# Attention scores of two heads side by side in the two halves of TensorE's rows, with six of nine part products, and weights staged outside the probabilities

## What is computed

```python
# attention, 16 heads of 8 channels, causal
q, k, v = x @ Wq.T, x @ Wk.T, x @ Wv.T            # split into heads
attn = softmax(where(causal, q @ k.T * 8 ** -0.5, -inf))
x = layernorm(x + (attn @ v) @ Wo.T)
# mixture of experts: 64 experts of inner width 64, 8 groups of 8
scores = sigmoid(x @ router_w.T); sfc = scores + e_bias
# sum of the top 2 of each group -> best 4 groups -> best 8 experts of those
w = scores[topk] / (sum + 1e-20) * 2.5            # coefficients, zero elsewhere
moe = sum_e ((silu(x @ Wg[e]) * (x @ Wu[e]) * coef[e]) @ Wd[e])
shared = (silu(x @ SWg) * (x @ SWu)) @ SWd        # inner width 128
x = layernorm(x + moe + shared)
```

## Time and profile before

| | before |
|---|---|
| median of 3 runs | 962.97 us (962.12 to 964.05) |
| the profiled execution's own time | 962.95 us |
| its span, from the first to the last instruction | 961.2 us |
| mean granted TensorE clock | 0.993 |
| busy: PE, DVE, ACT, POOL | 98%, 78%, 49%, 62% of the span |

### The profile page before, as it was taken

One profiled execution on the slowest core, in us unless ns is written; L12 is line 12 of the kernel. 1 busy time (PEld: TensorE's weight loads), 2 busy tenths in 40 slices (PEclk: granted clock), 3 DMA queues, 4 the chain that ended last, 5 costly groups with the idle time before them and its releaser, 6 DMA issues.

```text
span 961.2 us, 16058 instructions
## 1 busy us (share of the span) xinstructions
PE 940.5 (98%) x5012; PEld 574.7 (60%) x5012; DVE 752.1 (78%) x2374; ACT 468.0 (49%) x866; POOL 597.8 (62%) x651
## 2 busy tenths in 40 slices
PE   9899999999999999999999999999999999999996
PEld 4355466666666666666666656666666655666663
DVE  4776877799877997789967997789877997478655
ACT  2355445455555545555455545555455555543221
POOL 2343147765777757776766757776676767775653
PEclk9799999999999999999999999999999999999999
DMA  8551144432643253423633345323634223242431
GB/s 287 171 160 62 49 158 138 135 107 87 205 133 116 91 182 114 135 78 114 214 125 101 105 159 160 111 81 97 211 112 124 93 103 113 88 144 77 160 109 55
DMA packets 64340, 121.70 MB, mean 127 GB/s; under 512 B 6656, under 2 KB 36224, under 8 KB 63744
## 3 DMA queue, kind: packets, MB, share of 16 engines
q1 hardware_dynamic: 64256, 120.67, 39.1%
HBM read 98.37 MB, written 22.02 MB: 125 GB/s over the span
## 4 chain that ended last, share of the span: by engine, by line
PE 85%; DVE 7%; DMA 3%; issue 2%; POOL 1%; ACT 1%; SPq 0%; POOLq 0%; DVEq 0%
PE acc L844 12%; PE ob L785 7%; PE sm L755 7%; PE st L773 7%; PE pg L714 6%; PE pu L714 6%; PE pg L716 5%; PE pg L715 5%; PE pu L716 5%; PE pu L715 5%; PE acc L710 4%; PE acc L829 3%; PE acc L831 2%; PE acc L830 2%; PE ob L797 2%
## 5 line engine op out<-in xcount | busy, mean ns | idle before, releaser
L958 POOL TENSOR_TENSOR hid<-hid,coef_b 128x512 f32<-128x512 f32 x240 | 309.4, 1291 | 158.5 <-DVE hid L1215 99.6
L1147 DVE CUSTOM_DVE_ANT_0 max_out<-sm,causal_sb 128x128 bf16<-128x128 f32 (+3 forms) x512 | 236.0, 485 | 58.0 <-PE sm L755 54.0
L907 ACT ACTIVATE hid<-pg 128x512 f32<-128x512 f32 x243 | 145.4, 598 | 209.7 <-PE pg L716 203.4
L879 ACT ACTIVATE probs<-st 128x512 f32<-128x512 f32 (+1 forms) x384 | 194.5, 525 | 93.6 <-PE st L773 90.3
L1206 DVE SCALAR_TENSOR_TENSOR hid<-hid,pg 128x512 f32<-128x512 f32 x243 | 165.3, 680 | 54.4 <-ACT hid L907 53.2
L1215 DVE TENSOR_TENSOR hid<-hid,pu 128x512 f32<-128x512 f32 x235 | 160.3, 682 | 40.7 <-PE pu L716 37.9
L962 POOL TENSOR_TENSOR hid_lo<-hid,hid_hi 128x512 fp32r<-128x512 f32 x112 | 144.4, 1290 | 64.9 <-ACT hid_hi L914 64.3
L944 POOL TENSOR_SCALAR_AFFINE_SELECT probs<-probs 128x256 f32<-128x256 f32 x256 | 98.4, 410 | 61.5 <-ACT probs L879 61.5
L755 PE MATMUL sm<-k_stack,q_stack 72*128 72x128 bf16 (+3 forms) x512 | 132.5, 308 | 3.0 <-DMA k_stack<-k_rows_dram 2.4
L773 PE MATMUL st<-q_stack,k_stack 96*128 96x512 bf16 (+3 forms) x512 | 128.6, 304 | 0.1
L714 PE MATMUL pg<-x_hi,wg_hi 128*128 128x512 f32 x240 | 126.5, 527 | 1.3 <-DVE hid L1206 0.9
(11 more groups left out here) (161 smaller groups left out, 1295.5 us busy)
## 6 DMA issues: line engine op xcount, KB each, us to landing
coef_b<-coef_dram SPq DMA_DIRECT2D x128, 512.0 KB, 3.9
q_rows_dram<-qk_parts SPq DMA_DIRECT2D x24, 384.0 KB, 3.4
k_rows_dram<-qk_parts SPq DMA_DIRECT2D x24, 384.0 KB, 3.6
q_stack<-q_rows_dram SPq DMA_DIRECT2D x64, 144.0 KB
k_stack<-k_rows_dram SPq DMA_DIRECT2D x64, 144.0 KB
xT_sb<-in_xT SPq DMA_DIRECT2D x8, 256.0 KB, 3.9
y<-in_x SPq DMA_DIRECT2D x8, 256.0 KB, 4.2
out<-out_sb SPq DMA_DIRECT2D x8, 256.0 KB, 2.4
```

What stands on the lines that cost most here:

```text
L879: act.activation(probs[:, h % HG, at:at + wide], st_bank[i % 2][:, 0:wide], ACT.Exp, scale=C ** -0.5).then_inc(exp_done, 1)
L907: act.activation(hid_of(n, i), gate_bank(n, i)[:, :], ACT.Tanh, scale=0.5).then_inc(tanh_done, 1)
L958: pool.tensor_tensor(hid_of(n, i), hid_of(n, i), coef_b[:, half % 2, j, :], ALU.mult)\
L1147: last = dve.tensor_tensor_reduce(out=max_out[:, seg.nth(BANK_SM, task) % 2, col:col + wide], in0=sm_of(seg, task)[:, col:col + wide], in1 ...
```

## The change

Three things are changed, and with them all the order tables.

**Six of nine products.** The products of the small parts with each other are left out: copies (0,1,2), (3,4), (5) of the q parts stand against (0,3,5), (1,4), (2) of the k parts. A head has 48 rows instead of 72, and 2 rows for the maxima. `store_part` makes seven stores of single or double copies instead of six of triple ones.

**Two heads side by side.** `q_stack` and `k_stack` are 128 rows: the even head of a pair in rows 0 to 49, the odd one in rows 64 to 113. A task `mx` or `st` is now of a pair (24 of each for a batch): for e = 0 and 1 a matmul of the rows of half e into bank e. Both banks are thus in use by one task, and the next such task waits for both (`sm_wait` with one ahead, `bank_free` without `banks=2`). VectorE and ScalarE do both banks in one task. `rs` is four DMAs instead of two, `mT` two instead of one.

**Weights.** They come in 11 chunks through the two halves of `coef_b` and through `x1`, and no more through `probs`; VectorE splits the first chunk, GpSimd the others. In batch 0 the tasks `g`, `u`, `d` wait for the split of the chunk that they need, `x1` waits for the last chunk in `x1`, the first `c` for all. The small weights are loaded at the fourth `rs` instead of the second. `FILL_START` is 36.

```diff
-SPLIT_BY_DVE = 3
-CHUNKS = 9
+SPLIT_BY_DVE = 1
+CHUNKS = 11
...
+Q_COPIES = ((0, 1, 2), (3, 4), (5,))
+K_COPIES = ((0, 3, 5), (1, 4), (2,))
+COPIES = 6
+STORES = 7
...
-FILL_BEFORE, FILL_START = 8, 62
+FILL_BEFORE, FILL_START = 8, 36
...
-        q_stack = sb("q_stack", [STACK, RING, S], BF16)
-        k_stack = sb("k_stack", [STACK, RING, S], BF16)
+        q_stack = sb("q_stack", [P, RING_PAIRS, S], BF16)
+        k_stack = sb("k_stack", [P, RING_PAIRS, S], BF16)
...
+        def sm_wait(eng, seg, task):
+
+            n = seg.nth(BANK_SM, task)
+            last = seg.last(BANK_SM, task)
+            ahead = 1 if task[0] == "mx" or last and last[0] == "mx" else 2
+            if n > ahead:
+                eng.wait_ge(sm_free, n - ahead)
...
                         for stack, dram in ((q_stack, q_rows_dram), (k_stack, k_rows_dram)):
-                            sp.dma_start(stack[0:QK_ROWS, 2 * j:2 * j + 2, :],
-                                         dram[par, :, :, :, hs].rearrange("a b c h t -> (a b c) h t"))\
-                                .then_inc(stacked[j], 16)
+                            for e in range(2):
+                                sp.dma_start(stack[HALF * e:HALF * e + QK_ROWS, j, :],
+                                             dram[par, :, :, 2 * i + e].rearrange("a c t -> (a c) t"))\
+                                    .then_inc(stacked[j], 16)
...
+                    if kind == "c" and (n, i) == (0, 0):
+                        sp.wait_ge(lo_done, CHUNKS - 1)
...
-                        bank_free(pe, seg, sm_free, BANK_SM, task, banks=2)
+                        sm_wait(pe, seg, task)
...
-                            mm = pe.matmul(sm[:, col:col + wide], q_stack[0:QK_ROWS, h % RING, qb * P:(qb + 1) * P],
-                                           k_stack[0:QK_ROWS, h % RING, 0:wide], start=True, stop=True)
+                            for e in range(2):
+                                rows = slice(HALF * e, HALF * e + QK_ROWS)
+                                mm = pe.matmul(sm_bank[e][:, col:col + wide],
+                                               q_stack[rows, j % RING_PAIRS, qb * P:(qb + 1) * P],
+                                               k_stack[rows, j % RING_PAIRS, 0:wide], start=True, stop=True)
...
-                        bank_free(pe, seg, exp_done, ("st",), task, banks=2)
+                        bank_free(pe, seg, exp_done, ("st",), task)
...
-                            mm = pe.matmul(st_bank[i % 2][:, col:col + wide], k_stack[:, h % RING, kb * P:(kb + 1) * P],
-                                           q_stack[:, h % RING, kb * P:S], start=True, stop=True)
+                            for e in range(2):
+                                rows = slice(HALF * e, HALF * e + QK_ROWS + MAX_PARTS)
+                                mm = pe.matmul(st_bank[e][:, col:col + wide],
+                                               k_stack[rows, j % RING_PAIRS, kb * P:(kb + 1) * P],
+                                               q_stack[rows, j % RING_PAIRS, kb * P:S], start=True, stop=True)
...
-                        if (n, i) == (0, 0):
-
-                            act.wait_ge(waiting_free, SPLIT_BY_DVE)
...
+                        for e in range(2):
+                            ins = act.activation(probs[:, (2 * j + e) % HG, at:at + wide], st_bank[e][:, 0:wide],
+                                                 ACT.Exp, scale=C ** -0.5)
+                        ins.then_inc(exp_done, 1)
...
+                    if kind == "x1" and (n, i) == (0, 0):
+                        dve.wait_ge(lo_done, last_in_x1)
```

More of the change, by code:

```diff
@@ L103 @@
[L103 to L111, removed]
+    "ld": (-98.17253,),
+    "q": (-70.80342,),
+    "k": (-58.23719,),
+    "v": (-51.94068,),
@@ L112 @@
+    "coefT": (1.71973,),
+    "c": (2.25398, 2.96534,),
 }
 SECOND = {
[L114 to L118, removed]
[14 rows of a table removed]
-    "mask": (-51.293, -47.529, -46.076, -45.517, -40.832, -35.645, -33.87, -32.974, -24.099, -23.934, -22.722,
[L134 to L137, removed]
@@ new lines @@
+    "v": (-36.20943,),
+    "ldtok": (-12.73866,),
+    "qsplit": (-40.5456, -40.12837,),
+    "ksplit": (-39.89728, -38.04269,),
[12 rows of a table added]
+    "mask": (-26.84157, -26.26793, -25.75034, -25.0302, -23.20886, -20.06697, -20.05696, -20.03131, -17.51049,
+        -17.36116, -15.5983, -15.38545, -11.3013, -10.95221, -10.63246, -10.4969,),
+    "attT": (-8.47419,),
+    "oproj": (-7.6374,),
+    "x1T": (-4.91164,),
+    "router": (-4.75291,),
+    "x1": (-5.88705, -5.56618, -5.49436, -5.46016,),
+    "ln": (-7.22913, -6.65218, -6.41214,),
@@ L184 @@
-    "coefT": (0.226,),
-    "c": (0.242, 1.86,),
+    "ld": (-65.79889,),
+    "q": (-58.99325,),
+    "k": (-57.81871,),
+    "v": (-54.42258,),
+    "ldtok": (-21.97914,),
+    "qsplit": (-57.91075, -57.83259,),
+    "ksplit": (-52.55714, -51.23217,),
[12 rows of a table added]
+    "mask": (-37.02618, -35.59804, -34.80114, -34.66682, -29.56424, -29.40928, -28.80164, -28.71944, -21.86965,
+        -21.68776, -21.50863, -21.29233, -17.03666, -15.42321, -15.09321, -14.79594,),
+    "attT": (-11.78642,),
+    "oproj": (-9.92362,),
@@ L223 @@
+    "attT": (-10.71942,),
+    "oproj": (-8.99426,),
+    "x1T": (-6.76199,),
+    "router": (-5.78768,),
+    "x1": (-7.85019, -7.76244, -7.38375, -7.12726,),
+    "ln": (-8.57646, -8.27491, -8.12057,),
+    "tk": (-5.39817, -5.22484, -5.14949, -4.6389, -4.01822, -3.82713, -3.60513, -3.39587, -3.26224, -3.07535,
+        -3.02177, -2.57872, -2.1501, -2.11798, -1.62024, -0.86934, -0.73934, -0.32364, -0.23005, -0.2262,),
+    "coefT": (0.55051,),
+    "c": (0.93377, 1.16928,),
 }
 EXPERTS_FIRST = {
[25 rows of a table removed]
@@ L379, in __init__ @@
         self.numbers = {}
[L380 removed]
+        for kinds in (BANK_SM, SINGLE_SM, BANK_O, LN, ("q", "k")) + tuple((k,) for k in {t[0] for t in tasks}):
             here = [t for t in tasks if t[0] in kinds]
@@ L607, in store_part @@
             def store_part(kind, par, p):
-                dst = q_rows_dram[par, p] if kind == "q" else k_rows_dram[par, :, p]
-                sp.dma_start(dst.rearrange("o c h t -> (c h) o t"),
-                             qk_parts[:, kind == "k", p, :].unsqueeze(1).to_broadcast([P, PARTS, S]))\
-                    .then_inc(parts_stored, 16)
+                rows, part = (q_rows_dram[par], 0) if kind == "q" else (k_rows_dram[par], 1)
+                to = (Q_COPIES if kind == "q" else K_COPIES)[p]
+                runs = [to] if kind == "q" or len(to) < PARTS else [to[0:2], to[2:3]]
+                for run in runs:
+                    step = run[1] - run[0] if len(run) > 1 else 1
+                    dst = rows[run[0]:run[-1] + 1:step]
+                    sp.dma_start(dst.rearrange("o c h t -> (c h) o t"),
+                                 qk_parts[:, part, p, :].unsqueeze(1).to_broadcast([P, len(run), S]))\
+                        .then_inc(parts_stored, 16)
             def tasks(seg):
@@ L619, in tasks @@
                         place = chunks[i][4]
-                        if i - 2 >= SPLIT_BY_DVE:
-                            sp.wait_ge(lo_done, i - 2 - SPLIT_BY_DVE + 1)
+                        before = [j for j in range(i) if chunks[j][4] == place]
+                        if before:
+                            sp.wait_ge(lo_done, before[-1])
                         sp.dma_start(chunks[i][3], chunks[i][0]).then_inc(split_in[place], 16)
@@ L640, in tasks @@
                         sp.dma_start(hid[:, 1, :], causal).then_inc(id_in, 16)
-                    if kind == "rs" and (n, i) == (0, 1):
+                    if kind == "rs" and (n, i) == (0, 3):
                         for dst, src in small:
```

270 lines of the change are left out of this document (128 added, 142 removed), and 324 rows, old and new, of tables (EXPERTS, EXPERTS_FIRST, EXPERTS_LAST, EXPERTS_SECOND).

## The result

The changed kernel takes 977.48 us (median of 4 runs, 973.43 to 978.51) against 962.55 us of the kernel before beside it: a ratio of 1.0146, interval 1.0114 to 1.0179. It is slower by 15 us; the forecast was 960, and 1000 and 895 the ends of the range, but its direction was faster.

The account below looks back on a forecast made before the run. PE was taken as the bound after the head, the chain's length in the head. Terms: -51.2 + 52.3 - 24.2 + 14.9 + 2.9 + 2 = -3.3 us against 962.95, so 960 us; range 895 to 1000.

Parts of the forecast that it names:

- Term 1: Score parts after the first expert product: two heads streaming at once leave 280 parts fewer at 0.183 us, -51.2 us.
- the rival of serial halves: Second matmul of every pair: the halves work one after the other, costing 61 us, 1021 us in all; chance 0.10.
- Term 2: Changes between whole-array work and score parts: 231 visits at 0.28 us against 414 runs at 0.03, +52.3 us.
- The price taken from PV's column tiles: Visit price from PV's entry 0.09 us late and exit 0.22 late, together 0.31; 0.28 taken for row halves.
- the rival of cheap visits: Changing between whole and half rows costs little: 895 to 935 us; chance 0.27.
- Term 3: Head: with batch 1's scores put behind, the first expert product starts at 97 instead of 121.25, -24.2 us.
- The first expert product follows at 97: End of the head: last PV at 83.8, 13 us more to x1_lo's end at 96.8, then the experts.
- hidden under PE: SP's queue: four stack transfers for two, 0.38 us each to issue, 1.5 for a pair of heads, at no cost.
- Term 4: Behind the first expert product: PE waits for the routing coefficients before unit 1's down product, +14.9 us.
- the small ones: One PV and transposes of batch 1 moved behind the first expert product, +2.9 us; single-buffered mx waits, +2 us.

## Why the prediction was wrong

The time lies in the range and has the other sign: the forecast was 3 us faster, it came 15 slower.

**Term 1, two heads at once: right.** Forecast 0.183 us saved for each part that is no longer alone, 0.177 measured; the rival of serial halves fell.

**Term 2, entering and leaving: right.** Forecast 0.28 us a visit against 0.03 of an ordinary part, 0.30 read from the rows above and 0.25 net between two kernels. The price taken from PV's column tiles holds for row halves; the rival of cheap visits fell. Terms 1 and 2 gave a steady batch that is shorter by 1.4 us.

**Term 3, when the experts can start: this step failed.** "The first expert product follows at 97": it came at 111.4, 14.4 us late. First mT at 32.0 instead of 30.3, then 17.3, 15.4 and 14.5 us from one mT to the next instead of 13.5, the last PV of batch 0 at 92.9 instead of 83.8, and 18.5 us from it to the experts instead of 13.2. The runs put three things in its place.

The first is the clock. Every step was priced at the full clock, and with the fillers cut from 244 to 96 (90 of them on record) and batch 1's parts gone, the granted clock in the head was 0.78. Fillers alone gave back 6.0 us. The pace itself was right: with them two groups take 13.2 us each, and where the kernel after was granted 1.00 (86.9 to 88.6 us), PE and ScalarE take their turns on the one pair of banks in 1.57 us a part, where the sum had 1.6:

```profile
86.98 0.39 PE L823 MATMUL st<-q_stack,k_stack 50*128 50x512 bf16 x2 [0.43 <-ACT probs L928]
88.55 0.39 PE L823 MATMUL st<-q_stack,k_stack 50*128 50x384 bf16 x4 [0.86 <-ACT probs L928]
```

So the 5.4 us of a second pair of banks were no error of the sum; they are mostly the microseconds of the clock, and for the rest a better design.

The second is the way from the last PV to the experts. The sum took 13 us of the 15.8 to x1_lo, and put the experts 0.2 behind it. In the kernel after, the router's products and two fillers stand between, and at half clock they take 2.3 us (109.12 to 111.43):

```profile
109.17 1.97 PE L853 MATMUL ob<-rw_sb,x1T 128*128 128x64 f32 x8 [0.93 <-DVE x_lo L1249]
111.43 0.99 PE L753 MATMUL pg<-x_hi,sgu_hi 128*128 128x512 f32 x1
```

In the kernel with one filler in alternating stretches it is 14.4 us to x1_lo's end and 1.2 from there, together 15.7 (89.7 to 105.4). Taking batch 1 out of the way saved about half of the 2.8 us that the sum counted, and the router had no term.

The third is SP's queue in the second group, which I passed over in one sentence ("hidden under PE") though the small weights were moved into it: moving them on made the second mT 1.1 us earlier, and with fillers and banks 3.7. 8 of the 14 us were given back by clock, banks and queue together; of the rest, 2.5 us lie behind the last PV, and the others are open.

**Term 4 and the small ones, the stage behind the head: nearly right.** The forecast for all that stands behind the first expert product was +20.9 us (-51.2 + 52.3 + 14.9 + 2.9 + 2); it is 864.6 less 840.0, +24.6. From x1_lo's end (109.12) to unit 1's down product (below) are 29.6 us where the sum had 28. That the sizes come so near is in part luck: the clock had no place in this sum either (below). That this is a loss of moved work, and not of the pairs, was in the sum; that VectorE's maxima of batch 1 hold up the routing was not shown, as moving them cost more.

```profile
138.19 0.64 PE L823 MATMUL st<-q_stack,k_stack 50*128 50x384 bf16 x4
138.75 0.79 PE L880 MATMUL acc<-hid_hi,wd_hi 128*128 128x512 f32 x1
```

The granted clock cost here too: 0.67 between 110 and 140 us, where it was 1.00 before, with 0.42 us from one 512-column product to the next (136.91 to 137.33) instead of 0.23.

So the sign hung on one step. Two large terms were right to within a tenth and cancelled; what was left was the head, where the sum counted 24 us that could only be had if nothing else became late.

## What to carry to other kernels

Running two products in two halves of the rows saves one product's streaming, and costs about 0.3 us each time that PE goes from whole rows to halves and back (both as measured here); with 512 columns at 0.22 us a visit must hold more than one pair to pay, so count visits, not products. Before a shorter chain is counted as gain, price it at the clock that the engine will be granted with what is then left for it to do, give every step between the ends of the chain a term of its own, and walk each queue that a moved transfer stands in. Where the order of all engines is one list, a part that is moved by rule can cost more than the move was to save, as in every run here that moved some.

## What was not expected of the hardware

The granted clock fell to half behind a stand of 3.07 us (17.1 to 20.2 us) and, with PE busy for 18.9 of the next 30 us, stayed there until some 55 us; with more fillers it came to 0.89 in the same stretch and to 1.00 in the next. And the price of a change between half and whole rows shows in the weight load: with whole rows the 128x128 load for the next product started at 502.90, under columns that streamed until 503.11; with halves it started at 501.47, 0.10 us behind the last columns.
